# Gathering padded expert blocks by sixteen accumulating DMAs, and making z remainders on TensorE

## The reference, cut to what matters

```python
# x: (64, 32, 512) = (B, C, T);  O = I = 512, rank 64, 64 codebook levels, 16 experts of 32 x 32
delta = lora_B @ lora_A * 0.5                     # (512, 512)
cb    = codebook / max(|codebook|)
scale = exp(scale_log)                            # one per output row and group of 128
norm  = (weight + delta) / scale
idx   = searchsorted((cb[:-1] + cb[1:]) * 0.5, norm)   # the codebook is not sorted
w_eff = ((cb[idx] - norm) + norm) * scale + delta
x = x + x @ w_eff.T
x = x + einsum('bct,bcd->bdt', x, experts[token])      # (32 x 32) expert per batch element
```

## Time and profile before

| | us |
|---|---|
| runs of the kernel | 96.48 (95.57 to 96.67, 3 runs) |
| the profiled execution | 95.03 |
| its span, first to last instruction | 93.2 |
| PE busy in it | 80.3 (86%), 392 instructions |
| DVE busy | 67.3 (72%), 153 |
| ACT busy | 31.3 (34%), 53 |
| POOL busy | 17.9 (19%), 17 |

### The profile page before, as it was taken

How to read it: one execution, slowest core, us unless ns; L and a number is a source line. 1 busy time by engine, 2 the same in 40 slices (tenths; PEclk the granted TensorE clock), 3 DMA queues, 4 the chain that set the end, 5 groups by cost and what they waited for, 6 DMA issues and landing times.

```text
span 93.2 us, 1128 instructions
## 1 busy us (share of the span) xinstructions
PE 80.3 (86%) x392; PEld 64.2 (69%) x392; DVE 67.3 (72%) x153; ACT 31.3 (34%) x53; POOL 17.9 (19%) x17
## 2 busy tenths in 40 slices
PE   3964995899999846199999599999999999999980
PEld 3952340978777744099888288888888888888870
DVE  0049999949999999999999999999999902000000
ACT  0600008056787737229212222221322222222230
POOL 6340050007334650925700000000000000000000
PEclk9999999999999999999999999999999999999999
DMA  0399999980000000000032120222211233212241
GB/s 1 84 276 359 391 388 386 389 316 18 0 0 0 0 0 0 7 0 0 0 120 100 53 76 2 111 112 112 112 47 65 112 120 112 93 50 82 112 169 56
DMA packets 5941, 10.33 MB, mean 111 GB/s; under 512 B 944, under 2 KB 1200, under 8 KB 5936
## 3 DMA queue, kind: packets, MB, share of 16 engines
q1 hardware_dynamic: 5488, 9.45, 28.3%
q0 software_dynamic: 144, 0.52, 1.4%
q10 hardware_dynamic: 304, 0.30, 1.2%
HBM read 6.07 MB, written 4.19 MB: 110 GB/s over the span
## 4 chain that ended last, share of the span: by engine, by line
DVE 47%; PE 40%; DMA 5%; issue 3%; DVEq 1%; ACT 0%; SPq 0%
PE lora_ps L307 35%; DVE acc L500 13%; DVE jump L486 11%; DMA slog<-in_scale_log 5%; DVE z_lo L454 5%; PE z_ps L307 3%; DVE norm L450 3%; DVE norm L440 2%; PE lora_ps L298 2%; DVE acc L492 1%; DVE turned_pick L429 1%; DVE eff L507 1%; DVE pick L427 1%; DVE tree L384 1%; DVEq L516 1%
## 5 line engine op out<-in xcount | busy, mean ns | idle before, releaser
L500 DVE TENSOR_TENSOR acc<-acc,jump 128x512 f32<-128x512 f32 x28 | 22.2, 793 | 0.1
L287 PE MATMUL z_ps<-blocks,x_sb 128*128 128x128 f32 x128 | 17.4, 295 | 4.9 <-DVE z_lo L454 3.7
L287 PEld LDWEIGHTS z_ps<-blocks,x_sb 128*128 128x128 f32 x128 | 16.5, 209 | 6.8 <-issue 6.8
L486 DVE TENSOR_SCALAR jump<-norm,top,top_step 128x512 f32<-128x512 f32 x32 | 19.8, 630 | 1.2 <-issue 1.2
L240 ACT ACTIVATE x_sb<-lora_ps 128x512 f32<-128x512 f32 x15 | 9.0, 600 | 31.5 <-PE lora_ps L307 31.5
L202 POOL TENSOR_TENSOR z_lo<-x_sb,z_hi 128x512 fp32r<-128x512 f32 x8 | 13.1, 1637 | 20.2 <-ACT x_sb L226 20.2
L307 PE MATMUL lora_ps<-z_lo,m_hi 128*128 128x512 f32 x60 | 16.4, 396 | 0.0
L307 PE MATMUL lora_ps<-z_hi,m_hi 128*128 128x512 f32 x60 | 16.1, 390 | 0.0
L307 PE MATMUL lora_ps<-z_hi,m_lo 128*128 128x512 f32 x60 | 16.1, 389 | 0.0
L224 ACT ACTIVATE z_hi<-z_ps 128x512 fp32r<-128x512 f32 x16 | 9.6, 598 | 10.8 <-PE z_ps L287 10.8
L307 PEld LDWEIGHTS lora_ps<-z_hi,m_hi 128*128 128x128 f32 x60 | 11.3, 188 | 2.4
(11 more groups left out here) (70 smaller groups left out, 56.6 us busy)
## 6 DMA issues: line engine op xcount, KB each, us to landing
x_sb<-in_x SPq DMA_DIRECT2D x8, 512.0 KB, 9.5
out<-x_sb SPq DMA_DIRECT2D x15, 256.0 KB, 2.4
w_sb<-in_weight SPq DMA_DIRECT2D x4, 256.0 KB, 6.5
out<-x_sb SPq DMA_DIRECT2D x2, 128.0 KB, 1.9
lbt_sb<-in_lora_bt ACTq DMA_DIRECT2D x1, 128.0 KB, 5.1
la_sb<-in_lora_a ACTq DMA_DIRECT2D x1, 128.0 KB, 6.3
cb_raw<-in_codebook ACTq DMA_DIRECT2D x1, 32.0 KB, 4.8
tok_sb<-in_tokens SPq DMA_DIRECT2D x1, 0.5 KB, 3.7
```

The lines of the kernel that those rows point to most:

```text
L287: last = nc.tensor.matmul(z_ps[r % Z_BANKS][:, g, :], x_sb[:, r, g * P:(g + 1) * P], blocks[:, r, :], start=True, stop=True)
L486: return run(V.tensor_scalar(jump[:, s], norm[:, u], top[:, s:s + 1], top_step[:, s:s + 1], ALU.is_gt, ALU.mult))
L500: a = run(V.tensor_tensor(acc[:], acc[:], jump[:, s], ALU.add))
```

## The change: what it does

The expert table is laid out on the host with zeros, so that a gathered row of 512 B is a whole row of a 128 x 128 block. POOL copies the identity into all 16 blocks and then issues 16 indirect DMAs that add 128 rows each onto one block. z is made and split in pairs of r over two banks (three slots of two): ACT copies `z_hi` of a pair in one instruction, PE adds minus the identity times `z_hi` onto the banks, and ACT copies what is left to `z_lo`. ACT scales the LoRA product into `delta`. DVE makes `wg` and `fixed` by additions, and POOL adds the identity to a diagonal block. The branch and the search over all levels move to POOL, behind the gathers. x and weight are loaded in mixed order once the tokens are there. Four output banks rotate.

```diff
 # SP
-            for u in range(OC): ... load w
-            sp.wait_ge(gather_started, 1)
-            for i in range(XD): ... load x
+            sp.wait_ge(tok_in, 16)
+            load_x(0); load_w(0); load_x(1); load_x(2); load_w(1); load_x(3); load_x(4)
+            load_w(2); load_w(3); load_x(5); load_x(6); load_x(7)     # one call a line in the source
 # POOL
-            nc.gpsimd.memset(blocks[:], 0.0)
-            nc.gpsimd.indirect_dma_start(pick[:], None, experts, ...)
-            nc.gpsimd.tensor_tensor(match[:], match[:], step_up ..., ALU.mult)
-            for r in range(1, RT, 2): ... z_lo = z_sb - z_hi
+            nc.gpsimd.iota(row_no[:], pattern=[[0, RT]], base=0, channel_multiplier=1)
+            nc.gpsimd.tensor_copy(blocks[:], ident[:] ... .broadcast_to([P, RT, P]))
+            pool.wait_ge(blocks_filled, 1)
+            pool.wait_ge(rows_known, 1)
+            for r in range(RT):
+                nc.gpsimd.indirect_dma_start(blocks[:, r], None, experts,
+                                             bass.IndirectOffsetOnAxis(ap=row_of[:, r:r + 1], axis=0),
+                                             compute_op=ALU.add).then_inc(blocks_in[r // 2], 16)
+            pool.wait_ge(levels_counted, 1)
+            used_levels = pool.value_load(count_i[0:1, 0:1], min_val=1, max_val=L)
+            add_identity(0)                        # waits for fixed_made 1, 128x128 addition
+            with pool.If(used_levels > SLOTS + 1): search_all(0)
+            pool.sem_inc(fixed_ready, 1)
+            for u in range(1, OC): add_identity(u)
+            with pool.If(used_levels > SLOTS + 1): ... search_all(1 to 3)
+            pool.sem_inc(fixed_ready, OC - 1)
 # ACT
+            minus_ident = -ident;  for each u: delta[:, u] = 0.5 * ps[:, LORA_BANKS[u]]
+            for p in range(PAIRS):
+                high_z(p)                          # 128 x 1024 from two banks
+                if p > 0:
+                    low_z(p - 1)                   # waits for less_high(p - 1)
+            high_m(0)
+            low_z(PAIRS - 1)
 # PE
+            lora(0); lora(1); lora(2)
+            pe.wait_ge(minus_ready, 1)
+            for p in range(PAIRS):
+                make_z(p)                          # waits for x_in[p], both gathers, z_lo of p - 3
+                if p == 0: lora(3)
+                else:      less_high(p - 1)        # 2 matmuls of 512 columns with minus_ident
+            turn(0)
+            less_high(PAIRS - 1)
             # product(0) waits for two z_lo pairs, product(1) for all eight
 # DVE
+            V.scalar_tensor_tensor(row_of[:], tok_sb[:], float(P), row_no[:], ALU.mult, ALU.add)
-            match = (top == key);  (L410)
-            pick diagonal, transpose, 2 copies into blocks  (L427, L429, L434)
+            few = (count <= 9);  slot_step = step * few
+            for s in range(SLOTS):                 # 8 instructions with an accumulator
+                V.scalar_tensor_tensor(match[:, s], key[:], top[:, s:s + 1], step_up[:],
+                                       ALU.is_equal, ALU.mult, accum_out=top_step[:, s:s + 1])
+            add_lora(0)
+            normalize(0)
+            need(slots_known)
+            quantize(0, {1: lambda: make_fixed(0)})
+            for u in range(1, OC): add_lora(u)
+            for u in range(1, OC): normalize(u)
+            for u in range(1, OC): make_fixed(u)
+            quantize(1, {3: lambda: low_m(0)})
+            quantize(2, {3: lambda: low_m(1)})
+            quantize(3, {3: lambda: low_m(2)})
             low_m(3)
```

More of the change, by code:

```diff
@@ L83, in build @@
         count = sb("count", [P, 1])
+        few = sb("few", [P, 1])
         count_i = sb("count_i", [P, 1], I32)
@@ L149, in build, with z_banks, z_bank, pair @@
         search_step = sem("search_step")
[L151 to L155, removed]
+        level_read = sem("level_read")
         HN = T // 2
-        N_OUT = OC * NB
+        def z_banks(p):
+            first = FIRST_Z_BANK + 2 * (p % Z_SLOTS)
+            return slice(first, first + 2)
+        def z_bank(r):
+            return ps[:, FIRST_Z_BANK + 2 * (r // 2 % Z_SLOTS) + r % 2].rearrange("p (g n) -> p g n", g=G)
+        def pair(zz, p):
+            return zz[:, :, 2 * p * P:2 * (p + 1) * P].rearrange("t g (s n) -> t s g n", s=2)
+        def out_bank(n):
+            return ps[:, OUT_BANKS[n % len(OUT_BANKS)]]
+        turn_bank = ps[:, TURN_BANK].rearrange("p (g o) -> p g o", g=G)
         block = ctx.enter_context(nc.Block())
@@ L200, in _ @@
[L200 to L203, removed]
+            nc.gpsimd.iota(row_no[:], pattern=[[0, RT]], base=0, channel_multiplier=1).then_inc(rows_numbered, 1)
+            pool.wait_ge(ident_ready, 1)
+            nc.gpsimd.tensor_copy(blocks[:], ident[:].rearrange("p (o n) -> p o n", o=1).broadcast_to([P, RT, P])
+                                  ).then_inc(blocks_filled, 1)
@@ new lines, in add_identity @@
+            def add_identity(u):
+                pool.wait_ge(fixed_made, u + 1)
+                own = fixed[:, u, u * P:(u + 1) * P]
+                need(run(nc.gpsimd.tensor_tensor(own, own, ident[:], ALU.add)))
+            pool.wait_ge(levels_counted, 1)
+            used_levels = pool.value_load(count_i[0:1, 0:1], min_val=1, max_val=L)
+            add_identity(0)
+            with pool.If(used_levels > SLOTS + 1):
+                search_all(0)
+            pool.sem_inc(fixed_ready, 1)
@@ L205, in _ @@
+            for u in range(1, OC):
+                add_identity(u)
+            with pool.If(used_levels > SLOTS + 1):
+                for u in range(1, OC):
+                    search_all(u)
+            pool.sem_inc(fixed_ready, OC - 1)
         @block.scalar
@@ L213, in _, with high_z, low_z, normalize @@
             nc.scalar.activation(warm_sb[:], ident[:, 0:1], ACT.Copy).then_inc(warm, 1)
[L215 to L231, removed]
+            nc.scalar.activation(minus_ident[:], ident[:], ACT.Copy, scale=-1.0).then_inc(minus_ready, 1)
+            for u in range(OC):
+                act.wait_ge(lora_ready, u + 1)
+                nc.scalar.activation(delta[:, u], ps[:, LORA_BANKS[u]], ACT.Copy, scale=LORA_SCALE
+                                     ).then_inc(delta_ready, 1)
+            def high_z(p):
+                act.wait_ge(z_ready, p + 1)
+                nc.scalar.activation(pair(z_hi, p), ps[:, z_banks(p)].rearrange("t s (g n) -> t s g n", g=G), ACT.Copy
+                                     ).then_inc(z_hi_ready, 1)
+            def low_z(p):
+                act.wait_ge(z_less_hi, p + 1)
+                nc.scalar.activation(pair(z_lo, p), ps[:, z_banks(p)].rearrange("t s (g n) -> t s g n", g=G), ACT.Copy
+                                     ).then_inc(z_lo_ready, 1)
+            def normalize(u):
+                act.wait_ge(scaled, 1)
+                act.wait_ge(wg_ready[u], 1)
+                for g in range(G):
+                    group = slice(g * P, (g + 1) * P)
+                    last = nc.scalar.activation(norm[:, u, group], wg[:, u, group], ACT.Copy, scale=rscale[:, u, g:g + 1])
+                last.then_inc(normed[u], 1)
             def high_m(u):
@@ L239, in copy_out @@
                 act.wait_ge(out_ready, n + 1)
[L240 to L247, removed]
+                nc.scalar.activation(out_sb[:, n], out_bank(n), ACT.Copy).then_inc(out_copied, 1)
+            for p in range(PAIRS):
[4 more added lines that the diff above has]
+            low_z(PAIRS - 1)
             for n in range(N_OUT - 1):
@@ L251, in _ @@
                     high_m(n // NB + 1)
[L252 to L255, removed]
+            for half in range(2):
+                act.wait_ge(out_ready, N_OUT + half)
+                nc.scalar.activation(out_sb[:, N_OUT - 1, half * HN:(half + 1) * HN], ps[:, LAST_BANKS[half], 0:HN],
+                                     ACT.Copy).then_inc(last_copied, 1)
         @block.tensor
@@ L276, in make_z @@
[L276 to L288, removed]
-                last.then_inc(z_ready, 1)
+                nc.tensor.matmul(ps[:, FIRST_Z_BANK, 0:P], ident[:], ident[:], start=True, stop=True)
@@ new lines, in lora, with make_z @@
+            def lora(u):
+                nc.tensor.matmul(ps[:, LORA_BANKS[u]], lbt_sb[:, u * P:(u + 1) * P], la_sb[:], start=True, stop=True
+                                 ).then_inc(lora_ready, 1)
+            def make_z(p):
+                pe.wait_ge(x_in[p], 16)
+                pe.wait_ge(blocks_filled, 1)
+                pe.wait_ge(blocks_in[p], 32)
+                if p == Z_SLOTS - 1:
+                    pe.wait_ge(delta_ready, OC)
+                if p >= Z_SLOTS:
+                    pe.wait_ge(z_lo_ready, p - Z_SLOTS + 1)
+                for r in (2 * p, 2 * p + 1):
+                    for g in range(G):
+                        last = nc.tensor.matmul(z_bank(r)[:, g], x_sb[:, r, g * P:(g + 1) * P], blocks[:, r],
```

(32 more changed lines are left out.)

285 lines of the change are left out of this document (137 added, 148 removed).

## The result

| | before | after |
|---|---|---|
| median of 4 runs each, us | 96.17 (95.57 to 96.67) | 98.69 (97.71 to 98.85) |
| ratio of the runs | | 1.025 (95%: 1.017 to 1.034) |
| profiled execution, its span | 95.03, 93.2 | 97.71, 95.9 |
| PE, DVE, POOL busy | 80.3, 67.3, 17.9 | 76.9, 57.2, 31.7 |

I forecast 89.5 with a range of 85.5 to 97.0: the time lies above it, and the kernel became slower where I had forecast faster. DVE lost 10 us of work. The execution became longer by 2.7 us all the same, and POOL is the engine that grew. The page after, in the parts that answer to the earlier trace rows and to the cost of a gather; first the slices of 2.4 us (with the granted clock), then groups by line (busy us, mean ns, idle before and its releaser).

A forecast was written before the change was run, and what follows sets the result against it. DVE's quantizer bounds the kernel until about 43 us, then PE; afterwards POOL's gathers set the first stage. PE's end at 83.7 plus 2.7 tail plus 1.8 gives 88.2, on the median scale 89.5 us, range 85.5 to 97.

The forecast's parts named there:

- I take 1.4: POOL's queue: issue time in us of one adding gather, between 1.11 and 2.22; 16 issues end at 27.4.
- my doubling bound: Upper bound for issuing one adding gather: 2.22 us, twice the plain 1.11, if the destination's read must be described too.
- My sign of being wrong: The prediction is wrong if, among other signs, a gather's issue is above 1.8 or below 1.1 us.
- Rival C: POOL's queue ahead of `fixed_ready(0)`: gathers bind, kernel slower; deciding point 1.83 us each, at 2.22 time 101.3 (102.9); chance 0.13.
- From `fixed_ready` to `m_lo`: DVE from 28.9 to 40.3 us: `eff` 1.2, nine instructions 5.4, then 4.8 in `quantize(1)` through `low_m(0)`.
- PE's rest behind `m_lo`: PE's products after `m_lo` at 40.3: 45.2 less 1.8 for eight earlier matmuls, so PE ends at 83.7 us.
- DVE's path up to `eff`: DVE's small chain ready at 13.0, addition and normalization to 14.2, `quantize(0)` 9.6 more: done at 23.8 us.
- z on PE: PE's z stage: first pair at 11.6 to 13.6, through at 34.6 to 36.6, product 0 at 36 to 38 us.
- Rival A: PE's z stage binds if an adding gather issues in 1.11: time 85.7 to 87.7, median scale 87 to 89; chance 0.27.
- Rival B: DVE and POOL block each other: DVE's small chain 7 us longer, time 91.6, median scale 93, up to 96; chance 0.20.
- Rival D: POOL's identity copy takes 6.6 us, gathers begin at 8.4 instead of 5.0: time 91.6 (93); chance 0.08.

## Why the prediction was wrong, step by step

The mechanism was seen and its price missed. The step that failed is the forecast's "I take 1.4, near the plain form, because rows and partitions are the same and only the operation differs", and with it that sixteen issues are 16 x 1.4 = 22.4 us, with nothing between them. They took 30.6: 1.91 each.

- **Issue of a gather.** From 4.76 to 35.36 the gathers took 8.2 us more than forecast. The largest part, 4.6, is the gap of 0.30 between two, which I put at nothing: there was only one gather before, and so no row of it. The issue itself, 1.55 for 1.4, is 2.4, and gathers that took longer than 1.55 are the last 1.2. The plain form issues in 0.945, so the addition costs 0.60 over it. That lies below my doubling bound, whose reason, the read of the destination, isn't tested. My sign of being wrong, an issue above 1.8, didn't show (1.55), because it left out the gap too. 8.2 us later, less 0.2 for the earlier start and 0.8 for a cheaper branch: `fixed_ready` at 36.1 instead of 28.9.
- **Rival C was the case.** It named the place, POOL's queue ahead of `fixed_ready(0)`, and the point, 1.83 a gather. It came out at 1.91 and 2.5% slower. I gave it 0.13; a price that only a plain form shows, taken 16 times in a row, deserved its upper half.
- **From `fixed_ready` to `m_lo`.** 11.4 forecast, 11.8 measured; POOL's identity additions of the other u fall beside the start of `quantize(1)`, whose first pieces took 1.21 and 0.86, where I had 0.92 and 0.66.
- **The stall was not free of consequences.** PE's rest behind `m_lo` was to be 43.4 and took 93.19 - 47.93 = 45.3: after 4.07 us without work PE ran from 49 to 52 at half its clock (granted 0.50), with two groups of four matmuls at 1.89 instead of 1.07. That is 1.9 us that I didn't have. The three together are 83.7 + 7.2 + 0.4 + 1.9 = 93.2; PE ended at 93.19.
- **DVE's path up to `eff`.** Forecast 23.8, measured 22.8: right, from an earlier scale load (4.27 for 5.85) less dearer selections (0.21 each, not 0.14).
- **z on PE.** The start at 11.6 to 13.6 was wrong (14.85). I had said that 64 KB "surely" land no later than the 6.8 of 512 KB; beside x the first two gathers took 7.3 and 8.0. This cost nothing at the end. The last two pairs waited 1.4 and 1.0 us for their gathers, of which two are issued in 3.7, so the stage ended at 41 and not at 34.6 to 36.6. Where gathers don't hold it (one gather) the stage took 20.5 for my 23, and the first product followed 23.0 behind its start, where I had 24.4.
- **Rival A** would have been the case with cheap gathers: without the addition 88.0 was measured in the profiled execution, just above its 85.7 to 87.7.
- **Rival B** fell: beside gathers comparisons took 0.54 (0.61 at most in `quantize(0)`), and the small chain ran through in 7.5 us, without one instruction over 0.52. What the runs show is the other direction: the gather waits. The Trainium skill, in "SBUF — State Buffer", section "Who interferes with whom", names copies and `tensor_scalar`, the form of the comparisons, as what can take the shared ports, and infers that `tensor_tensor` doesn't stall descriptor generation. The measurement differs from that inference, and decides: nine `tensor_tensor` with both inputs in SBUF and without a gap stretched a gather to 6.16, while beside `quantize(0)`, where comparisons and such additions alternate, none took over 2.20. That it is the shared ports isn't shown here.
- **Rival D** was excluded: the identity copy took 1.89 and was over at 3.4.
- **** I read a little wrong: PE's unbroken row of 9 starts in the 24th slice, not the 23rd, and DVE is at 9 from the 4th to the 32nd but for the 9th. No term came from it.

Not tried: the remainders on TensorE against the old way by themselves, the branch on POOL by itself, and one-input DVE instructions without a gap beside a gather.

## What to carry to other kernels

A queue that issues many small indirect DMAs is an engine with a price per instruction: multiply the dearest bound by the count, add the gap between two, and look for what another engine waits for behind them. Moving that forward alone gained nothing here, since the data of the last gathers came later still; fewer gathers did. When a large edit comes as a parcel, undo the suspicious part alone before judging the rest: here one part turned a gain of 6.5% into a loss. And when a stall is moved, look at what the freed engine now runs beside.

## What the runs showed of the hardware

- An adding indirect DMA of 128 rows of 512 B issues in 1.55 us, a plain one in 0.945, with 0.30 between two of either. The first of a row took 1.70 and 1.13, a single plain one of 4 KB rows 1.09 to 1.11.
- A gather in issue was held for 4.6 us more (1.55 to 6.16) beside nine two-input DVE instructions without a gap; with waits between them, which cost DVE 0.1 us each, the longest took 2.11.
- Behind the loads of x a 64 KB gather landed 3.1 to 3.3 us after the start of its issue, once 4.8; beside the 512 KB loads it took up to 8.0 (up to 8.9 in the version with the branch moved).
- After 4.07 us without work PE ran its first four 512-column matmuls in 1.21 us and the next eight in 1.89 for each four, at a granted clock of 0.50, against 1.07 from 53 us on, when the granted clock was full again.
